# Delta attention and a mixture with slots: where the first passes prepare weights and slots, and where two tiles of maxima stand

## The chip, the cores and the metric

The kernel runs on one core of one Trainium2 chip. The metric is the time of one execution on the device in microseconds. Engines are TensorE (PE in the profile), VectorE (DVE), ScalarE (ACT), GpSimd (POOL) and SyncE (SP), which only issues DMAs here.

## What is computed

```python
# attention, on layer-normed x: 4 sequences of 2048 tokens, D = 256, C = 128
k = k / max(norm(k), 1e-12)
trans = a_t * (I - b_t * kkT)
S = einsum('bij,bjk->bik', S, trans) + b_t * vkT
o = einsum('bc,bcd->bd', q_t, S) * g_t
x = x + (o @ Wo + bo)
# mixture of 8 x 128 slots, on layer-normed x
xn = rms_norm(x, gamma_x);  se = rms_norm(slot_embeds, gamma_slot)
logits   = einsum('bsd,etd->bset', xn, se)
dispatch = softmax(logits, axis=1)          # over the tokens
slots    = einsum('bsd,bset->betd', xn, dispatch)
processed = gelu(slots @ w1) @ w2
combine  = softmax(logits.reshape(b, s, e * t), axis=-1)
x = x + einsum('bnd,bsn->bsd', processed, combine)
```

## The kernel before

The attention works on 16 chunks of 128 tokens, each for all four sequences at once. Within a chunk the recurrence becomes a triangular system: M of a chunk is the product of its keys with themselves, scaled by decays (`system`, L582 on VectorE, its matmuls L1137 on TensorE). M goes to DRAM and comes back repeated over partitions (`blocks_out`, `blocks_in` on SyncE), and VectorE solves its diagonal blocks of 16 columns in 15 pairs of small operations (`product`, L596, and `column`, L607), which I call the base system. GpSimd spreads the result into Z (`spread_blocks`, L464), and three doublings on TensorE, ScalarE and VectorE (`turn_Z`, `products`, `doubling`, L621 and L624) complete the inverse. From it come the updates, the next state, the scores and the outputs.

Every engine has its own order of work, written out by hand in a function `step(i, q)`, called for i from -4 to 15. One step takes a base system of chunk i + 2, M of chunk i + 3, the projections of chunks i + 3 and i + 4, outputs of chunk i + 1 and the normed result of chunk i. `steps` unrolls i = -4 to -1, runs i = 0 to 11 in a hardware loop of six times two steps, and unrolls 12 to 15; with `first=1` it unrolls 0 and 1 too. An engine works strictly in its order; between engines semaphores hold it. `at` is i where it is a number of Python, and so in the unrolled steps alone.

VectorE's step consists of a first part with the base system, in between which stand biases (L555), weights, next states and the gated product (L645), and of a tail: input statistics, residual (L655), decays by scans (L564, L571), M (L582), the first doubling, the low part `Xl` of the normed result (L686), right side, second doubling, statistics, low parts of the turned input (L548) and the last doubling. GpSimd's step starts once M of a chunk is there: residual addition (L414), a cut of M by a mask (L448), decayed keys kTg (L436) and queries qTg (L443), the other cut, a half cut (L456), then small norms, Z (L464) and the spread of beta (L430).

The mixture's weights are prepared within attention's first steps, on VectorE. `mixture_weights(1)` scales w1 by gamma (step -3), `(2)` writes the high fp16 part of w2 (step -3, L700), `(3)` that of w1 and `(4)` the low part of w2 (step -2, ahead of the base system, L703 and L706), `(5)` the low part of w1 (tail of step -2, L710). `slots_scaled` scales the eight groups of slot embeddings by their norms and gammas (L718), `slots_high` casts them to fp16 (L724); both stand ahead of the base system of step -1, and `slots_low` (L728) in its tail. The slots are turned on TensorE in step 13.

At the end, TensorE computes the first half of batch 0's logits in steps 14 and 15 and after (`early_logits`), ScalarE copies them out of PSUM into L (L1061), and VectorE takes column maxima `cmax` and row maxima `rmax` of each tile of 128 tokens (`early_maxima`, L846, L849, L850): tiles 0 to 2 in the tail of step 15, tiles 3 to 15 after the last step. The mixture goes on with the second half of the logits; it turns `cmax` on TensorE (L1923), reduces it on VectorE (`m_mcol`, L1591) and spreads it on TensorE (L1929).

## Time and profile before

| | us |
|---|---|
| median of three runs (1187.94, 1190.2, 1190.31) | 1190.2 |
| the profiled execution | 1187.25 |
| its span, first to last instruction | 1185.4 |
| TensorE busy | 1113.2 (94%) |
| VectorE busy | 938.2 (79%) |
| ScalarE busy | 735.6 (62%) |
| GpSimd busy | 314.5 (27%) |
| mean granted clock of TensorE | 0.985 of full speed |

All times of rows are microseconds from the start of the span. The timeline lists an engine's instructions in their order; a bracket behind one tells how long the engine stood idle before it, and what released it. A duration contains what the instruction waits for within the engine, so that the same operation can have several durations. An end is a start and a duration added.

### The profile page before, as it was taken

The page shows a single profiled execution, that of the slowest core. Times are in us where ns is not written, and L with a number is a line of the kernel's source. Part 1 is how long each engine was busy: PE and PEld are TensorE (multiplying, and loading weights), DVE is VectorE, ACT ScalarE, POOL GpSimd, SP SyncE. Part 2 cuts the span into 40 slices and gives each one's busy share as a digit, 9 for nine tenths or more (in the row PEclk, how much of TensorE's full clock was granted, in tenths as well). Part 3 has the DMA queues.
Part 4 walks back from the last instruction along what each step waited for, and adds up shares of the span by engine and source line. Part 5 has one row for each costly group of instructions (what it writes and reads, how often), then busy time and mean ns, then how long its engine had stood idle before and what let it go on. Part 6 is the DMA issues. An engine that isn't in the chain of part 4 may idle for free.

```text
span 1185.4 us, 26905 instructions
## 1 busy us (share of the span) xinstructions
PE 1113.2 (94%) x8600; PEld 854.5 (72%) x8600; DVE 938.2 (79%) x2195; ACT 735.6 (62%) x1385; POOL 314.5 (27%) x389
## 2 busy tenths in 40 slices
PE   4489999999999889899999999999999999999998
PEld 2378888888888764587786486787486787487787
DVE  4789888888889747997586898576898666998665
ACT  3446567665766445687663697664587664497763
POOL 3647656676567611000021000022000022000012
PEclk9699999999999989999999999999999999999999
DMA  6113432233233343232273031264031355000155
GB/s 191 45 45 81 125 98 85 87 107 119 80 88 95 99 96 100 66 72 57 55 170 78 2 72 45 63 147 103 2 72 32 74 123 130 0 1 1 22 119 128
DMA packets 185519, 94.02 MB, mean 79 GB/s; under 512 B 123680, under 2 KB 176928, under 8 KB 185440
## 3 DMA queue, kind: packets, MB, share of 16 engines
q1 hardware_dynamic: 178384, 75.40, 26.6%
q0 software_dynamic: 5792, 17.05, 4.9%
q8 instruction: 49, 0.80, 0.3%
q10 hardware_dynamic: 1264, 0.53, 0.2%
q14 instruction: 30, 0.25, 0.1%
HBM read 38.42 MB, written 29.36 MB: 57 GB/s over the span
## 4 chain that ended last, share of the span: by engine, by line
PE 66%; DVE 16%; issue 11%; ACT 4%; POOL 2%; DMA 1%; DVEq 1%; SPq 0%; ACTq 0%; POOLq 0%
PE m_wide L2015 14%; PE m_wide L1992 7%; PE m_wide L1978 7%; PE m_wide L1898 6%; PE a_bank L1095 4%; DVE m_Dm L1598 3%; PE a_bank L1107 3%; PE a_bank L1157 2%; DVE m_El L1606 2%; PE m_wide L2003 2%; ACT m_Eh L1781 2%; PE a_bank L1233 2%; PE a_bank L1146 2%; DVE cmax L1569 2%; PE m_wide L1952 2%
## 5 line engine op out<-in xcount | busy, mean ns | idle before, releaser
L1536 POOL DMA_DIRECT2D out_dram<-m_o x64 | 35.4, 553 | 627.1 <-DVE m_o L1720 514.3
L1952 PE MATMUL m_wide<-m_X,m_Eh 128*128 128x257 f16 (+1 forms) x1024 | 171.5, 273 | 2.7 <-DVE m_El L1606 2.7
L1898 PE MATMUL m_wide<-seT,XT 128*128 128x512 f16 x672 | 147.3, 379 | 0.9 <-issue 0.8
L2015 PE MATMUL m_wide<-m_Ph,m_Th 128*128 128x257 f16 x512 | 140.4, 274 | 4.3 <-DVE m_Pl L1645 4.3
L1952 PE MATMUL m_wide<-m_X,m_El 128*128 128x257 f16 (+1 forms) x512 | 139.7, 273 | 0.0
L2015 PE MATMUL m_wide<-m_Ph,m_Tl 128*128 128x257 f16 x512 | 139.4, 272 | 0.0
L2015 PE MATMUL m_wide<-m_Pl,m_Th 128*128 128x257 f16 x512 | 139.1, 272 | 0.0
L1898 PEld LDWEIGHTS m_wide<-seT,XT 128*128 (+1 forms) x672 | 65.5, 98 | 78.5 <-ACT L L1754 1.5
L1952 PEld LDWEIGHTS m_wide<-m_X,m_Eh 128*128 128x128 f16 x1024 | 99.2, 98 | 20.8 <-DVE m_El L1606 3.8
L1754 ACT COPY L<-m_wide 128x512 f32<-128x512 f32 (+1 forms) x112 | 65.1, 584 | 78.6 <-PE m_wide L1898 77.8
L1774 ACT ACTIVATE m_E<-m_Dm,m_eshift 128x512 f32<-128x512 f32 x128 | 92.5, 722 | 23.5 <-DVE m_Dm L1598 22.5
L1817 ACT COPY m_Tl<-m_wide 128x1024 f16<-128x1024 f16 x64 | 64.7, 1011 | 66.1 <-PE m_wide L2003 66.1
L1606 DVE TENSOR_TENSOR m_El<-m_E,m_Eh 128x512 f16<-128x512 f32 x128 | 87.7, 688 | 7.2 <-ACT m_Eh L1781 3.3
L1598 DVE TENSOR_TENSOR m_Dm<-L,m_Mb 128x512 f32<-128x512 f32 x128 | 87.6, 684 | 0.0
L1569 DVE TENSOR_TENSOR cmax<-cmax,L 128x512 f32<-128x512 f32 x112 | 77.1, 689 | 9.7 <-ACT L L1754 6.3
L1992 PE MATMUL m_wide<-w2s,m_hh 128*128 128x256 f16 x512 | 84.5, 273 | 0.0
L1978 PE MATMUL m_wide<-m_sTh,w1s 128*128 128x512 f16 x256 | 77.5, 379 | 0.0
L1781 ACT CAST m_Eh<-m_E 128x512 f16<-128x512 f32 x128 | 77.0, 605 | 0.0
L1575 DVE TENSOR_REDUCE rmax<-L 128x1 f32<-128x512 f32 (+1 forms) x112 | 76.0, 679 | 0.0
L1811 ACT ACTIVATE L<-L,m_nrm (+1 forms) x64 | 73.7, 1151 | 0.9 <-DVE m_nrm L1640 0.9
L1992 PE MATMUL m_wide<-w2s,m_hl 128*128 128x256 f16 x256 | 69.8, 273 | 0.0
L1631 DVE TENSOR_TENSOR m_hl<-m_E,m_hh 128x512 f16<-128x512 f32 x64 | 43.9, 691 | 24.6 <-ACT m_hh L1802 24.5
(198 smaller groups left out, 2712.5 us busy)
## 6 DMA issues: line engine op xcount, KB each, us to landing
L<-in_L_attn_x_dram SPq DMA_DIRECT2D x16, 512.0 KB, 7.2
Mrep<-M_dram SPq DMA_DIRECT2D x32, 256.0 KB
x_dram<-x SPq DMA_DIRECT2D x16, 512.0 KB, 6.6
m_X<-X_dram SPq DMA_DIRECT2D x128, 64.0 KB, 1.8
m_x1t<-x_dram POOLq DMA_DIRECT2D x32, 256.0 KB, 3.5
out_dram<-m_o POOLq DMA_DIRECT2D x64, 128.0 KB, 2.4
M_dram<-M_ SPq DMA_DIRECT2D x16, 256.0 KB, 2.6
X_dram<-Xh SPq DMA_DIRECT2D x16, 256.0 KB, 2.3
```

Of the source, the lines that this page charges most:

```text
L1569: dve.tensor_tensor(cmax[:, half_at], cmax[:, half_at], L[:, z, bass.ds(tile, 1), :] .rearrange("q a n -> q (a n)"), ALU.max).then_inc(cm_ ...
L1575: dve.tensor_reduce(rmax[:, bass.ds(z * NT + tile, 1)], L[:, z, bass.ds(tile, 1), :] .rearrange("q a n -> q (a n)"), AX.X, ALU.max, negate ...
L1598: dve.tensor_tensor(Dm[p][:, :], L[:, v, bass.ds(4 * g + t, 1), :] .rearrange("q a n -> q (a n)"), Mb[:, v * HS:(v + 1) * HS], ALU.subtrac ...
L1606: dve.tensor_tensor(El[t % 4][:, :], E[t % 4][:, :], Eh[t % 4][:, :], ALU.subtract)\
L1774: act.activation(E[t % 4][:, :], Dm[p][:, :], ACT.Exp, bias=eshift[:, 0:1]).then_inc(E_ok[p], 1)
L1781: act.copy(Eh[t % 4][:, :], E[t % 4][:, :]).then_inc(Eh_ok[p], 1)
L1811: act.activation(row, row, ACT.Exp, bias=nrm[:, bass.ds(4 * k + t, 1)]).then_inc(Ec_ok, 1)
L1898: last = pe.matmul(lg[t % 4], XT[:, sx * KD + k, bass.ds((4 * g + t) * P, P)], seT[:, ss, k, z * HS:(z + 1) * HS], start=(c == 0), stop=(c ...
L1952: last = pe.matmul(acc[v][q], e[t % 4][:, qs], X[:, sx, bass.ds(4 * g + t, 1), 0:XW].rearrange("q a n -> q (a n)"), start=first and e is E ...
L1978: last = pe.matmul(up[f % 2], w1s[:, sw, k, f * P:(f + 1) * P], sT[ss][:, k, :], start=(c == 0), stop=(c == 3 * KD - 1))
L1992: last = pe.matmul(down[q % 2], hT[sh][:, f, q * P:(q + 1) * P], w2s[:, sw, f, :], start=(c == 0), stop=(c == 3 * NF - 1))
L2015: last = pe.matmul(co[p], a, pp[:, e, 0:XW], start=(c == 0), stop=(c == 3 * NS - 1))
```

## The change

On GpSimd, the low part of w2 is made at the end of step -3 (`second_weights_low`: w2 is scaled in place, and its high part subtracted); in step -2 the key norms and the spread of beta of chunk 1 come ahead of and behind the residual addition instead of near the end. On VectorE, `mixture_weights(4)` is gone, `(3)` stands behind the decays of step -2, the scaled slots stand in two halves of four in the tails of steps -1 and 0, the high part in the tail of step 1, and the low part in that of step 12. Its steps 0 and 1 are unrolled. On ScalarE and TensorE the keys and the system of chunk 1 come ahead of Z of chunk 0 in step -2. The memset and tile 0 of the maxima stand behind the weights in step 14, tile 1 behind the gated product, and tiles 2 to 5 in the tail of step 15.

```diff
--- before.py
+++ after.py
@@ -478,8 +478,14 @@
             def step(i, q):
                 r = 1 - q
                 at = i if isinstance(i, int) else None
+                if at == -2:
+                    if live(i + 3):
+                        key_norms(i + 3)
                 if live(i + 2):
                     residual(i + 2, q)
+                if at == -2:
+                    if live(i + 3):
+                        spread_beta(i + 3)
                 if live(i + 2):
                     cut(i + 2, q, 1)
                 if live(i + 2):
@@ -491,16 +497,23 @@
                     half_cut(i + 2, q)
                 if live(i):
                     output_norm(i)
-                if live(i + 3):
+                if live(i + 3) and at != -2:
                     key_norms(i + 3)
                 if live(i + 2):
                     spread_blocks(i + 2, q)
-                if live(i + 3):
+                if live(i + 3) and at != -2:
                     spread_beta(i + 3)
                 if live(i + 4):
                     norm(i + 4)
                 if at == -3:
+                    second_weights_low()
                     slot_norms()
+
+            def second_weights_low():
+                pool.wait_ge(w2h_ok, 1)
+                pool.tensor_scalar(w2_in, w2_in, WSCALE, None, ALU.mult).then_inc(w2h_ok, 1)
+                pool.wait_ge(w2h_ok, 2)
+                pool.tensor_tensor(w2s[:, 1, :, :], w2_in, w2s[:, 0, :, :], ALU.subtract).then_inc(w2h_ok, 1)
 
             def slot_norms():
                 pool.wait_ge(sq_ok, 1)
@@ -701,23 +714,21 @@
                 elif step == 3:
                     dve.wait_ge(w1_ok, 1)
                     dve.tensor_copy(w1s[:, 0, :, :], w1_g).then_inc(w1_ok, 1)
-                elif step == 4:
-                    dve.wait_ge(w2h_ok, 1)
-                    dve.scalar_tensor_tensor(w2s[:, 1, :, :], w2_in, WSCALE, w2s[:, 0, :, :],
-                                             ALU.mult, ALU.subtract)
                 elif step == 5:
                     dve.wait_ge(w1_ok, 2)
                     dve.tensor_tensor(w1s[:, 1, :, :], w1_g, w1s[:, 0, :, :], ALU.subtract).then_inc(w1_ok, 1)
 
-            def slots_scaled():
-
-                dve.wait_ge(srn_ok, 1)
-                dve.wait_ge(w1_ok, 3)
-                dve.wait_ge(gxs_ok, 1)
-                for e in range(NS):
+            def slots_scaled(first, past):
+                if first == 0:
+                    dve.wait_ge(srn_ok, 1)
+                    dve.wait_ge(w2h_ok, 3)
+                    dve.wait_ge(w1_ok, 3)
+                    dve.wait_ge(gxs_ok, 1)
+                for e in range(first, past):
                     last = dve.scalar_tensor_tensor(slots_g[:, e, :], slots_in[:, e, :], srn[:, e:e + 1], gxs[:, :],
                                                     ALU.mult, ALU.mult)
-                last.then_inc(slots_ok, 1)
+                if past == NS:
+                    last.then_inc(slots_ok, 1)
 
             def slots_high():
                 dve.wait_ge(slots_ok, 1)
@@ -748,11 +759,6 @@
                         biases(i + 3, r, 3)
                     if live(i + 3):
                         biases(i + 3, r, 1)
-                    mixture_weights(3)
-                    mixture_weights(4)
-                if at == -1:
-                    slots_scaled()
-                    slots_high()
                 for s in range(BS - 1):
                     if live(i + 2):
                         product(i + 2, s)
@@ -767,6 +773,8 @@
                     if s == 8:
                         if live(i + 1):
                             weights(i + 1, r)
+                        if at == NCH - 2:
+                            early_maxima(0)
                     if s == 10:
                         if live(i + 1) and live(i + 2):
                             next_state(i + 1, r, 0)
@@ -778,6 +786,8 @@
                     if s == 12:
                         if live(i + 1):
                             gated(i + 1, r)
+                        if at == NCH - 2:
+                            early_maxima(1)
                 if live(i + 2):
                     columns_done(i + 2)
                 if live(i + 4):
@@ -801,6 +811,8 @@
                     decays(i + 3, r, 1)
                 if at == -3:
                     mixture_weights(2)
+                if at == -2:
+                    mixture_weights(3)
                 if live(i + 3):
                     system(i + 3, r)
                 if live(i + 3):
@@ -812,9 +824,15 @@
                 if at == -2:
                     mixture_weights(5)
                 if at == -1:
+                    slots_scaled(0, NS // 2)
+                if at == 0:
+                    slots_scaled(NS // 2, NS)
+                if at == 1:
+                    slots_high()
+                if at == NCH - 4:
                     slots_low()
                 if at == NCH - 1:
-                    for t in range(3):
+                    for t in range(2, 6):
                         early_maxima(t)
                 if live(i):
                     low_part(i)
@@ -849,8 +867,8 @@
                 dve.tensor_tensor(cmax[:, 0:HS], cmax[:, 0:HS], L[:, 0, t, :], ALU.max).then_inc(cm_ok, 1)
                 dve.tensor_reduce(rmax[:, t:t + 1], L[:, 0, t, :], AX.X, ALU.max, negate=True).then_inc(rm_ok, 1)
 
-            steps(dve, step)
-            for t in range(3, NT):
+            steps(dve, step, first=1)
+            for t in range(6, NT):
                 early_maxima(t)
 
         @block.scalar
@@ -1014,11 +1032,14 @@
                     keys(i + 3, r)
                 if live(i + 3):
                     gates(i + 3, r)
+                if at == -2:
+                    if live(i + 3):
+                        turned_keys(i + 3)
                 if live(i + 2):
                     turned_Z(i + 2, 0)
                 if at == NCH - 3:
                     turned_slots((0,))
-                if live(i + 3):
+                if live(i + 3) and at != -2:
                     turned_keys(i + 3)
                 if live(i + 2):
                     products(i + 2, 0)
@@ -1274,17 +1295,23 @@
                     outputs(i + 1, at == NCH - 2)
                 if live(i + 3):
                     spread_alpha(i + 3)
+                if at == -2:
+                    if live(i + 3):
+                        turn_keys(i + 3, r)
+                if at == -2:
+                    if live(i + 3):
+                        system(i + 3)
                 if live(i + 2):
                     turn_Z(i + 2, q, 0)
                 if at == NCH - 3:
                     turn_slots((0,))
-                if live(i + 3):
+                if live(i + 3) and at != -2:
                     turn_keys(i + 3, r)
                 if live(i + 2):
                     products(i + 2, q, 0)
                 if at == NCH - 3:
                     turn_slots((1,))
-                if live(i + 3):
+                if live(i + 3) and at != -2:
                     system(i + 3)
                 if live(i + 2):
                     doubling(i + 2, q, 0)
```

## Rows read from the trace of the kernel before

**Rows 1.** The page, part 4: the chain that ended last, by engine.
```profile
PE 66%; DVE 16%; issue 11%; ACT 4%; POOL 2%; DMA 1%; DVEq 1%; SPq 0%; ACTq 0%; POOLq 0%
```

**Rows 2.** VectorE's timeline, 27 to 53 us: start, duration, engine, line, operation.
```profile
27.03 1.20 DVE L700 TENSOR_SCALAR w2s<-seT 128x2048 f16<-128x2048 f32 x1
...
37.60 1.22 DVE L703 CAST w1s<-L 128x2048 f16<-128x2048 f32 x1
38.74 4.44 DVE L706 SCALAR_TENSOR_TENSOR w2s<-seT,w2s 128x2048 f16<-128x2048 f32 x1
43.10 1.27 DVE L596 TENSOR_TENSOR tmp<-Mrep,a_const 128x60 f32<-128x60 f32 x1
44.41 1.19 DVE L607 TENSOR_TENSOR Zc<-a_const,tmp 128x60 f32<-128x60 f32 x1
...
47.41 0.21 DVE L596 TENSOR_TENSOR tmp<-Mrep,Zc 128x52 f32<-128x52 f32 x1
...
52.99 0.17 DVE L607 TENSOR_TENSOR Zc<-Zc,tmp 128x4 f32<-128x4 f32 x1
```

**Rows 3.** VectorE's timeline, 59 to 74 us.
```profile
59.38 0.69 DVE L582 TENSOR_TENSOR M_<-a_bank,gamb_ 128x512 f32<-128x512 f32 x1 [2.25 <-PE a_bank L1137]
...
61.60 2.27 DVE L710 TENSOR_TENSOR w1s<-L,w1s 128x2048 f16<-128x2048 f32 x1
...
69.15 3.24 DVE L718 SCALAR_TENSOR_TENSOR L<-XT,srn,gxs 128x256 f32<-128x256 f32 x8
...
73.57 0.21 DVE L596 TENSOR_TENSOR tmp<-Mrep,a_const 128x60 f32<-128x60 f32 x1
```

**Rows 4.** GpSimd's timeline beside the first base system.
```profile
40.99 3.31 POOL L448 TENSOR_TENSOR L<-M_,a_const 128x512 f32<-128x512 f32 x1
44.26 1.26 POOL L436 TENSOR_TENSOR kTg_<-kT,gbc_ 128x512 f32<-128x512 f32 x1
```

**Rows 5.** Stretches: length, each engine's busy time, TensorE's clock, DMA share, GB/s.
```profile
38.00:38.50 0.50, 0.50 (x4) 0.26 (x3) 0.50 (x1) 0.50 (x5) 0.50 (x2) 1.00 0.03 8
78.70:82.10 3.40, 3.40 (x16) 3.14 (x15) 2.34 (x13) 0.87 (x3) 1.26 (x2) 0.50 0.00 0
```

**Rows 6.** GpSimd's timeline in the tail of step -1.
```profile
89.00 2.37 POOL L414 TENSOR_TENSOR L<-L,bo 128x1024 f32<-128x1024 f32 x1
```

**Rows 7.** VectorE's timeline in later steps.
```profile
82.55 0.69 DVE L645 TENSOR_TENSOR OT<-a_bank,gateT_ 128x512 f32<-128x512 f32 x1 [1.34 <-PE a_bank L1224]
...
91.25 2.27 DVE L728 TENSOR_TENSOR L<-L 128x2048 f16<-128x2048 f32 x1
...
116.04 2.29 DVE L686 TENSOR_TENSOR Xl<-xf,Xh 128x1024 f16<-128x1024 f32 x1
...
406.19 1.20 DVE L686 TENSOR_TENSOR Xl<-xf,Xh 128x1024 f16<-128x1024 f32 x1
...
409.58 0.42 DVE L621 TENSOR_TENSOR Z_<-Z_,a_bank 128x256 f32<-128x256 f32 x1 [0.95 <-PE a_bank L1170]
```

**Rows 8.** TensorE's timeline in step -1.
```profile
77.53 0.39 PE L1107 MATMUL a_bank<-L,wqg_h 128*128 128x512 f16 x1 [3.87 <-DVE L L555]
```

**Rows 9.** VectorE's timeline in steps 14 and 15.
```profile
449.70 0.69 DVE L645 TENSOR_TENSOR OT<-a_bank,gateT_ 128x512 f32<-128x512 f32 x1 [3.68 <-PE a_bank L1224]
451.95 1.45 DVE L655 TENSOR_TENSOR x<-L,a_bank 128x512 f32<-128x512 f32 x2 [1.57 <-PE a_bank L1233]
...
456.89 0.91 DVE L846 MEMSET cmax<- 128x1024 f32 x1 [0.16 <-issue]
...
461.88 1.22 DVE L686 TENSOR_TENSOR Xl<-xf,Xh 128x1024 f16<-128x1024 f32 x1 [0.29 <-ACT Xh L973]
```

**Rows 10.** TensorE's timeline at the start of the mixture.
```profile
478.10 0.66 PE L1923 MATMUL m_wide<-ident,cmax 128*128 128x128 f32 x4 [1.61 <-DVE cmax L849]
...
484.07 0.65 PE L1929 MATMUL m_wide<-ident,m_mcol 128*128 128x128 f32 x4 [1.43 <-DVE m_mcol L1591]
```

## The prediction

> **What bounds the kernel now.** I read the page first. Its chain of the work that ended last lies on TensorE for 66% of the span and on VectorE for 16% [rows 1]. Then I went through attention in order of time, engine by engine. The attention part is a pipeline of 20 steps, of 24.2 us each once it runs (from Xl at 116.04 to Xl at 406.19 in twelve). From step 0 on VectorE hardly rests in one, so an edit counts where it lengthens or shortens VectorE's series of work. The first steps run otherwise. In step -2 VectorE's first base system starts at 43.10, behind a cast and a 4.44 us operation [rows 2]. In step -1 the second one starts at 73.57, behind 4.4 us of slot work from 69.15 on [rows 3]. In the first the reader is to see two late starts, in the second a wait on TensorE of 2.25 us before M of chunk 1 at 59.38.
>
> The rows of GpSimd beside these [rows 4] show what I take to decide the case. VectorE's operation at 38.74 needs some 2.2 us (the one of the same size at 61.60 took 2.27 [rows 3]) and took 4.44: it began to run at about 41.0, where GpSimd's addition ended and its cut was issued, and ended at 43.18. That cut, 1.26 us of work as the kTg behind it, took 3.31 us and ended at 44.30. VectorE's product of 60 columns took 1.27 us instead of 0.21 (at 47.41 [rows 2]) and ended 0.07 us later, at 44.37; the column update behind it took 1.19 us and ended at 45.60, just after GpSimd's kTg. Two more follow in the same way. So two operations that both read two operands of SBUF exclude each other, and a waiting one gets its turn as soon as the other engine's single operation ends. Operations of VectorE that take one operand from PSUM, and the statistics, run through. The pairs give two prices: after GpSimd's operation VectorE's ends its own length less 0.13 us later (0.07 for 0.21), and then GpSimd's of 512 elements ends some 1.13 us later (43.18 to 44.30).
>
> **Step -3 and -2.** Removed ahead of the first base system: the cast (1.2 us) and the low part of w2 (4.44 us). It can start at 37.7, where the cast did; its matrix is there by then but for its end, for the DMA engines fall silent at 38 [rows 5]. GpSimd now scales w2 (2048 elements, one operand) and subtracts. No row has that size there: from the addition's 1024 elements in 2.37 us [rows 6] the subtraction is some 4.6 us, the scaling between 2 us (half of the rate of the same row) and 4.6 us. The first starts once the high part is written, at 28.2 (27.03 and 1.20 us [rows 2]), and the second ends between 35 and 37.6. In that stretch each operation of VectorE has an operand in PSUM (M, the scans, low parts and biases), so I cost them at nothing; if they took 2 us more, they would hold the first base system by as much. The Trainium skill (Perfetto Trace Analysis, Optimizing Scalar/DVE Operations) says that moving work between VectorE and GpSimd may not help, for they share a port. By that rule up to 4.6 us would come back here; by the rows, with nothing of two SBUF operands beside it, none does.
>
> GpSimd's key norms of chunk 1 now stand ahead of its addition. They wait for ScalarE's four squares, which start when VectorE's last bias is done at 37.6; with a maximum and a power behind them I put 2.7 us for all, an estimate, so that the addition starts at about 40.3. Where it starts moves little: it blocks VectorE for the same time. Queued behind it are the spread of beta, two cuts, kTg and a half cut: 2.25 + 4 x 1.13 + 0.6, a good 7.5 us with VectorE's turns. The base system needs 6.75 us alone (26 operations from 47.41 to 53.16 and the first four at 0.25). During the 7.5 us it gets one operation in after each of six, 1.4 us of work. So it ends at 37.7 + 6.75 + 6.1 = 50.6 instead of 53.16: 2.6 us gained out of 5.6 removed. Z of chunk 0 goes with it.
>
> Keys and system of chunk 1 now run on TensorE while it waits for that Z, and its wait of 2.25 us on M goes. The 6.2 us from 53.16 to 59.38 become 6.2 - 2.25 + 1.2 (the cast) = 5.1, so M of chunk 1 comes at 55.7, 3.7 us sooner. SP's store and the two broadcasts follow it and are no wait. VectorE's last w1 part then meets GpSimd's addition or cut, and ends at about 61.1 instead of 63.87 [rows 3]: 2.8 us sooner. The doubling behind it moves along.
>
> **Step -1.** The slot scaling and the high part (69.15 to 73.57, 4.4 us) leave the place ahead of the second base system. It starts at 69.15 - 2.8 = 66.4, which is 7.2 us sooner. The wait of 1.34 us for the gated product at 82.55 [rows 7] came from TensorE being late (its wait of 3.87 us [rows 8], then 1.2 GHz for 3.4 us [rows 5]) and goes too. That makes -8.5 at the end of this base.
>
> In the tail the low slot part (2.27 us, 91.25) gives way to four scalings. Each takes 0.405 us alone (3.24 for eight [rows 3]), and each has two SBUF operands. They arrive as GpSimd's addition ends (89.00 + 2.37 = 91.37 [rows 6]), with a cut, kTg, qTg and a cut queued. The four end at 91.37 + 4 x 0.27 + 3 x 1.13 = 95.84 against 93.52: +2.3.
>
> **Step 0.** The other four stand ahead of Xl (116.04 [rows 7]), which took 2.29 us instead of 1.20 (406.19) since it waited for a cut, and ended at 118.33. So that cut ended 1.07 us before, at 117.26. From there four times 0.27, four operations of GpSimd (3 x 1.13 and a half cut's 0.5) and Xl's 1.07 give 123.3: +4.9. If they come just ahead of the cut, 4.4.
>
> **Step 1.** The cast of the slots (1.2 us, by the one at 37.60) and one GpSimd operation that gets in before Xl: +2.3; I take +2.0, since a short wait of VectorE behind it, as the one of step 12 below, can take up a little.
>
> **Step 12.** The low slot part (2.2 us) ahead of Xl (406.19), then kTg, then Xl: Xl ends at 410.6 instead of 407.39. VectorE waited 0.95 us at 409.58 [rows 7], so +2.3. No wait later in attention absorbs it: what follows hangs on that doubling.
>
> Alone, without GpSimd in between, these four places cost -0.6, +1.6, +1.2 and +1.3. The bounds of each are these and the above.
>
> **Clock.** TensorE now idles 5 to 6 us in the tail of step 0. In the trace an idle stretch of 3.87 us was followed by 3.4 us at 1.2 GHz [rows 5, 8], which cost the 1.34 us above. I take one such stretch: +1.3; bounds 0 and four.
>
> **The maxima.** The memset and tile 0 now run after the weights, tile 1 after the gated product of the last chunk: VectorE's waits of 3.68 us at 449.70 and of 1.57 us at 451.95 [rows 9] hide the 2.1 and 1.2 us. In the last step memset and three tiles fill 456.89 to 461.6 (0.9 and 3.7 us, so 1.2 a tile), and four tiles end at 461.7, just before the wait of 0.29 us on Xh is over. So ten instead of thirteen tiles remain after Xl, 1.2 us each: 3.6 us. TensorE waits for them at 478.10 (1.61 us) and for the column maxima at 484.07 (1.43 us) [rows 10] and is full from there on. So it gets 3.0 of the 3.6: -3.0.
>
> **Sum.** -8.5 + 2.3 + 4.9 + 2.0 + 2.3 + 1.3 - 3.0 = +1.3. The profiled execution took 1187.25 us (span 1185.4), so it would take 1188.5. The median of the runs shown is 2.95 us higher; on that scale it is 1191.5. A measurement of this kernel can tell 0.2%, 2.4 us, from nothing. This is within it.
>
> **Rivals.**
> *The scalings keep the port.* They follow each other with no semaphore, and GpSimd may not get in between. For it: no row shows back-to-back operations of one line against GpSimd. Against: the addition got in between the cast and the 4.44 us operation, which also stood back to back. Then the four places cost the lower figures and no gap opens that lowers the clock: -8.5 - 0.6 + 1.6 + 1.2 + 1.3 - 3.0 = -8.0, or 1182.2. The Trainium skill (SBUF — State Buffer, Who interferes with whom) says that whoever starts first has the shared pair for the whole instruction and the other blocks. It does not say who is next; read for a series it would give this time. The trace agrees on the lock (4.44 us at 38.74). Chance 0.32.
> *Slower: the clock.* The tails of steps -1, 0, 1 and 12 all open gaps of some 2 us or more on TensorE; if each is followed by a stretch at 1.2 GHz for 1.34 us, the sum is +1.3 + 3 x 1.34 = +5.3, or 1195.5. It decides from the second on. Against it: each gap but step 0's is shorter than the 3.87 us. Chance 0.09.
> *GpSimd's w2 part isn't hidden:* at the rate of its cut it runs past 37.7, and the first base system starts up to 2 us later: +3.3, or 1193.5. Chance 0.05.
>
> **Chances and range.** My forecast has 0.54, its own range is 1187 to 1195: 0.05 of it faster by over 0.2%, 0.32 within, 0.17 slower. With the rivals: faster 0.05 + 0.32 = 0.37; within 0.32 + 0.02 = 0.34; slower 0.17 + 0.09 + 0.03 = 0.29. The range takes in the first rival and the slow one: 1181 to 1195.5.
>
> **What would show it.** Right: the first base system starts near 37.7 and ends near 50.6 with six stretched operations; M of chunk 1 near 55.7; the second base system near 66.4; scalings of some 1.4 us from one to the next with GpSimd's between; no wait on cmax at TensorE. Wrong: scalings 0.4 us apart; a base system that ends before 49 or after 52; 1.2 GHz in other tails; a wait on XT or L in place of the one on cmax.

## The result, and the profile after

The changed kernel took 1197.07 us (median of four runs, 1196.84 to 1197.58) beside 1189.92 us of the kernel before: a ratio of 1.0069, interval 1.0053 to 1.0085. That is 7.15 us slower, and 1197.07 lies outside my range of 1181 to 1195.5. The profiled execution of it took 1197.58 us, with a span of 1196.0 us. That is 10.6 more than the span profiled before, which came from one of the faster runs of that kernel.

The page after, part 1 (busy time) and part 4 (the chain that ended last, by engine):

```profile
PE 1123.4 (94%) x8600; PEld 863.4 (72%) x8600; DVE 946.3 (79%) x2194; ACT 736.8 (62%) x1385; POOL 324.5 (27%) x391
...
PE 71%; DVE 13%; issue 8%; ACT 4%; POOL 3%; DMA 1%; DVEq 0%; ACTq 0%; SPq 0%; POOLq 0%
```

TensorE is busy 10.2 us longer than before, with the same matmuls to do, and its share of the chain went from 66% [rows 1] to 71%. The same multiplications took longer. The view of stretches says where. I cut attention where a base system starts, so that each row is one step. First the kernel before, then the changed one. The columns are length, busy time of TensorE, weight loads, VectorE, ScalarE and GpSimd (number of instructions in brackets), TensorE's granted clock, DMA share and GB/s.

```profile
43.10:73.57 30.47, 18.55 (x144) 16.45 (x144) 24.52 (x66) 10.58 (x25) 18.97 (x18) 0.78 0.20 59
73.57:99.42 25.85, 20.90 (x148) 17.21 (x148) 22.70 (x77) 10.63 (x30) 15.24 (x15) 0.93 0.23 62
99.42:124.24 24.82, 23.61 (x188) 19.95 (x186) 22.16 (x77) 15.47 (x40) 15.36 (x18) 1.00 0.31 88
124.24:148.46 24.22, 23.70 (x189) 19.99 (x187) 21.57 (x77) 15.48 (x40) 15.56 (x18) 1.00 0.34 102
```

```profile
36.19:67.57 31.38, 21.37 (x124) 17.47 (x125) 24.37 (x58) 10.38 (x29) 24.42 (x22) 0.73 0.23 59
67.57:95.99 28.42, 25.02 (x186) 20.77 (x184) 24.30 (x80) 12.85 (x35) 14.52 (x15) 0.93 0.24 66
95.99:129.48 33.49, 27.52 (x186) 22.65 (x185) 27.14 (x81) 15.51 (x40) 15.00 (x18) 0.81 0.25 71
129.48:158.43 28.95, 26.67 (x187) 22.24 (x186) 23.71 (x78) 15.52 (x40) 15.86 (x18) 0.88 0.28 83
158.43:183.16 24.73, 23.52 (x186) 19.76 (x184) 22.06 (x77) 15.60 (x40) 15.32 (x18) 1.00 0.29 82
```

The reader is to see steps 0 and 1 (third and fourth row). They ran at a clock of 1.00 before and run at 0.81 and 0.88 now. TensorE is busy 3.9 and 3.0 us longer in them with as many matmuls, and they last 8.67 and 4.73 us longer. The whole difference of the two spans, in such stretches:

| stretch | before | after | difference | predicted |
|---|---|---|---|---|
| start to VectorE's last bias before chunk 0 | 37.69 | 36.27 | -1.42 | 0 |
| from there to the second base system | 35.88 | 31.30 | -4.58 | -7.2 |
| step -1 | 25.85 | 28.42 | +2.57 | +1.0 |
| step 0 | 24.82 | 33.49 | +8.67 | +6.2 |
| step 1 | 24.22 | 28.95 | +4.73 | +2.0 |
| step 2 | 24.01 | 24.73 | +0.72 | 0 |
| steps 3 to 11 | 217.44 | 217.42 | -0.02 | 0 |
| step 12 | 23.52 | 26.98 | +3.46 | +2.3 |
| step 13 to the first turn of cmax | 64.66 | 65.21 | +0.55 | -1.6 |
| from there to the end | 707.33 | 703.24 | -4.09 | -1.4 |
| sum | | | +10.6 | +1.3 |

VectorE's timeline after, which answers to [rows 2, 3, 7]:

```profile
36.19 0.25 DVE L609 TENSOR_TENSOR tmp<-Mrep,a_const 128x60 f32<-128x60 f32 x1
...
53.81 0.69 DVE L595 TENSOR_TENSOR M_<-a_bank,gamb_ 128x512 f32<-128x512 f32 x1
...
56.98 0.42 DVE L634 TENSOR_TENSOR Z_<-Z_,a_bank 128x256 f32<-128x256 f32 x1 [1.84 <-PE a_bank L1191]
...
67.57 0.21 DVE L609 TENSOR_TENSOR tmp<-Mrep,a_const 128x60 f32<-128x60 f32 x1
...
83.90 4.68 DVE L728 SCALAR_TENSOR_TENSOR L<-XT,srn,gxs 128x256 f32<-128x256 f32 x4
...
113.71 5.72 DVE L728 SCALAR_TENSOR_TENSOR L<-XT,srn,gxs 128x256 f32<-128x256 f32 x4
119.35 1.63 DVE L699 TENSOR_TENSOR Xl<-xf,Xh 128x1024 f16<-128x1024 f32 x1
...
148.69 2.29 DVE L699 TENSOR_TENSOR Xl<-xf,Xh 128x1024 f16<-128x1024 f32 x1
...
419.02 2.29 DVE L699 TENSOR_TENSOR Xl<-xf,Xh 128x1024 f16<-128x1024 f32 x1
```

GpSimd's timeline after: the two new operations on w2, and what stood beside the scalings at 83.90 (it answers to [rows 4, 6]).

```profile
26.82 5.39 POOL L514 TENSOR_SCALAR seT<-seT 128x2048 f32<-128x2048 f32 x1
32.28 4.08 POOL L516 TENSOR_TENSOR w2s<-seT,w2s 128x2048 f16<-128x2048 f32 x1
...
83.97 1.52 POOL L448 TENSOR_TENSOR L<-M_,a_const 128x512 f32<-128x512 f32 x1
85.45 1.45 POOL L436 TENSOR_TENSOR kTg_<-kT,gbc_ 128x512 f32<-128x512 f32 x1
86.86 1.44 POOL L443 TENSOR_TENSOR qTg_<-qT_,gbc_ 128x512 f32<-128x512 f32 x1
88.26 1.44 POOL L448 TENSOR_TENSOR L<-M_,a_const 128x512 f32<-128x512 f32 x1
```

Four scalings of 0.405 us each take 4.68 and 5.72 us. Beside them GpSimd's operations follow each other every 1.4 us, one after each scaling. That is the alternation I had forecast, and the rival in which the scalings keep the port is out. By the port I mean whatever makes two operations that both read two operands of SBUF exclude each other, as in these rows.

TensorE's timeline after: step -2, the tails of steps -1, 0, 1 and 12, and the start of the mixture (it answers to [rows 10]).

```profile
46.36 2.07 PE L1158 MATMUL a_bank<-kT 128*128 128x128 f32 x8 [4.46 <-ACT kT L943]
...
90.81 0.66 PE L1167 MATMUL a_bank<-a_const,Z_ 128*128 128x128 f32 x4 [3.11 <-DVE Z_ L634]
...
123.21 1.12 PE L1167 MATMUL a_bank<-a_const,Z_ 128*128 128x128 f32 x4 [5.70 <-DVE Z_ L634]
...
153.21 0.93 PE L1167 MATMUL a_bank<-a_const,Z_ 128*128 128x128 f32 x4 [2.02 <-DVE Z_ L634]
...
422.95 1.01 PE L1167 MATMUL a_bank<-a_const,Z_ 128*128 128x128 f32 x4 [2.75 <-DVE Z_ L634]
...
492.77 0.60 PE L1950 MATMUL m_wide<-ident,cmax 128*128 128x128 f32 x4
...
497.09 0.60 PE L1956 MATMUL m_wide<-ident,m_mcol 128*128 128x128 f32 x4
```

Eight matmuls took 2.07 us behind an idle stretch of 4.46 us, and four took 1.12 behind 5.70, where the same four took 0.66 in the step before. Behind the gaps of 2.02 and 2.75 us they took 0.93 and 1.01. The turns of cmax and of the column maxima no longer have a bracket: they wait for nothing that the profile shows.

### The profile page after: what moved, and what is told of

Read it like the earlier page. It is cut to its first block, busy times and chain, and to the rows that moved or that the text cites. A ratio compares the mean times of both kernels' runs of the same rounds, so it can differ in the third digit from the quotient of the medians.

```text
span 1196.0 us, 26871 instructions
## 1 busy us (share of the span) xinstructions
PE 1123.4 (94%) x8600; PEld 863.4 (72%) x8600; DVE 946.3 (79%) x2194; ACT 736.8 (62%) x1385; POOL 324.5 (27%) x391
## 4 chain that ended last, share of the span: by engine, by line
PE 71%; DVE 13%; issue 8%; ACT 4%; POOL 3%; DMA 1%; DVEq 0%; ACTq 0%; SPq 0%; POOLq 0%
PE m_wide L2042 14%; PE m_wide L1925 11%; PE m_wide L2019 7%; PE m_wide L2005 7%; PE a_bank L1116 4%; DVE m_Dm L1625 3%; PE a_bank L1128 3%; DVE m_El L1633 2%; PE m_wide L2030 2%; ACT m_Eh L1808 2%; PE a_bank L1178 2%; PE a_bank L1254 2%; PE a_bank L1167 2%; PE m_wide L1979 2%; PE a_bank L1218 1%
```

## The experiments

My theory once the traces were there: the port terms are right, and the loss beyond them is TensorE's clock, which stands at 1.2 GHz behind the gaps that the scalings make. The rivals were the amount of work itself and w2 on GpSimd. The kernels ran on several chips, so I compare each with the kernel before on its own chip by the ratio, and the steps by the traces. Where I give microseconds under the changed kernel, they are plain differences of medians, across chips. The lengths of steps, with the time in them at 1.2 GHz in brackets, for the kernels below (us; the first column runs from the end of the last bias to the second base system, and holds 4.4 us of slot work in before, e1, e4, e6 and e12):

```
kernel              to step -1    step -1       step 0        step 1        step 12       to the end*
before              35.88 (13.7)  25.85 (3.4)   24.82 (0)     24.22 (0)     23.52         771.99
after               31.30 (17.1)  28.42 (4.0)   33.49 (13.0)  28.95 (6.9)   26.98         768.45
e9_after_again      30.94 (17.1)  28.45 (3.4)   31.05 (6.8)   27.30 (3.4)   27.09         768.12
e5_no_maxima        31.24 (17.1)  28.44 (3.9)   33.48 (13.0)  28.96 (7.0)   26.92         770.99
e4_maxima_only      36.55 (13.6)  26.79 (6.8)   24.83 (0)     24.22 (0)     23.51         768.89
e12_maxima_again    37.17 (17.1)  25.63 (3.4)   24.80 (0)     24.21 (0)     23.96         770.81
e1_slots_back       36.36 (17.1)  26.48 (6.8)   24.63 (0)     23.81 (0)     23.66         768.46
e6_step_m2_only     36.38 (17.1)  24.43 (0)     24.66 (0)     23.81 (0)     24.25         769.59
e2_slots_in_base    31.18 (17.1)  25.25 (0)     25.19 (0)     24.72 (0)     25.92         768.35
e10_in_base_again   31.09 (17.1)  25.24 (0)     25.19 (0)     24.71 (0)     25.94         769.03
e3_filler           31.03 (17.1)  26.93 (0)     29.51 (0)     25.81 (0)     26.63         766.92
e7_filler_m2        28.64 (3.4)   25.24 (0)     25.19 (0)     24.73 (0)     26.03         770.15
e8_half_in_tail     30.60 (17.1)  25.24 (0)     32.09 (10.2)  25.42 (3.4)   25.50         766.71
e11_low_early       31.29 (17.1)  25.24 (0)     25.19 (0)     28.45 (3.4)   23.52         767.45
                    * from the start of the last base system (step 13)
```

**e1: the slots back ahead of step -1's base system**, the low part in its tail; all else as changed.

```
-                if at == -1:
-                    slots_scaled(0, NS // 2)
...
+                if at == -1:
+                    slots_scaled(0, NS)
+                    slots_high()
                 for s in range(BS - 1):
```

> The changed kernel with the slot work put back: all eight scalings and the high part ahead of the base system of step -1, the low part in the tail of step -1; all else as changed. My theory: the loss sits in the slot work, which in the tails alternates with GpSimd's operations (3.1, 4.5, 1.1 and 1.1 us of waiting by the changed trace) and opens gaps on TensorE that are followed by 1.2 GHz. So the second base system starts 4.4 us later than in the changed kernel, but the two stretches at 1.2 GHz after 92 and 119 are gone, and the time falls by about 10 us, to 2 or 3 us under the kernel before (the maxima's 2 to 3 us, with next to nothing from step -2). Rival, the reordered step -2 or VectorE's unrolled steps are at fault: the time stays within 3 us of the changed kernel. Rival, it is the mere amount of VectorE work in the later tails: the same fall of 10 us, so this run alone doesn't tell it from mine; the run with the slots in the base does.

Measured: 1181.55 us, ratio 0.9928 (0.991 to 0.9945), 15.5 us under the changed kernel. Steps 0 and 1 are back at 24.63 and 23.81 us. The loss sits in the moved slot pieces. I had expected a fall of 10 us. Between the two profiled executions it is 15.4 us: 14.2 from the last bias to the last base system, 1.2 in the load, and nothing behind.

**e2: the four pieces inside the base systems** of the same steps, behind their second column, where GpSimd is idle. The work on VectorE is the same, the neighbour is not.

```
+                    if s == 1:
+                        if at == -1:
+                            slots_scaled(0, NS // 2)
+                        if at == 0:
+                            slots_scaled(NS // 2, NS)
+                        if at == 1:
+                            slots_high()
+                        if at == NCH - 4:
+                            slots_low()
```

> The changed kernel with each of the four pieces of slot work in the same step but inside the base system, behind its second pair of operations, where GpSimd stands idle. VectorE does the same work in the same step. My theory (the port): four scalings take 1.6 us instead of 4.7 and 5.7, the cast 1.2, the low part 2.2, Xl 1.2 or 2.3; no gap of more than 1 us ahead of TensorE's second turn of Z. The four pieces cost 1.6 + 1.6 + 1.2 + 2.2 = 6.6 us where they cost some 20 now, so the time falls by 10 to 13 us, to 3 to 6 us under the kernel before. Rival, the amount of work: nothing but the place within a step has changed, so the time stays within 3 us of the changed kernel. Rival, the gaps only move (TensorE waits for the weights' product instead) and are followed by 1.2 GHz as well: the waits of VectorE go but 1.2 GHz stays in steps 0 and 1, and the fall is 6 us or less.

Measured: 1181.03 us, ratio 0.9922 (0.9902 to 0.9942). VectorE's timeline, and the stretches of steps -1, 0 and 1:

```profile
69.06 1.67 DVE L728 SCALAR_TENSOR_TENSOR L<-XT,srn,gxs 128x256 f32<-128x256 f32 x4
```

```profile
68.12:93.36 25.24, 23.91 (x187) 19.72 (x185) 21.46 (x80) 12.92 (x35) 13.29 (x15) 1.00 0.23 62
93.36:118.56 25.20, 23.93 (x187) 19.79 (x185) 22.79 (x82) 15.47 (x40) 15.32 (x18) 1.00 0.31 89
118.56:143.28 24.72, 23.86 (x186) 19.72 (x184) 22.78 (x79) 15.47 (x40) 16.38 (x18) 1.00 0.29 86
```

Four scalings take 1.67 us instead of 4.68 and 5.72, the clock stays at 1.00, and steps 0 and 1 are 8.3 and 4.2 us shorter than in the changed kernel. So the amount of work isn't the cause. Alternation and clock together are; what each is worth, the next one tells. By its ratio e2 is no faster than e1: both undo the loss, and the slots gain nothing from their new places.

**e3: unused matmuls in TensorE's gaps.** The changed kernel, with 26, 50 and 16 matmuls of 256 columns into a free part of a bank ahead of the third turn of Z in steps -1, 0 and 1. They add no result. TensorE's steps 0 and 1 are unrolled for it, which no run tests by itself.

```
+                if at in (-1, 0, 1):
+                    filler({-1: 26, 0: 50, 1: 16}[at])
                 if live(i + 2):
                     turn_Z(i + 2, q, 2)
```

> The changed kernel with matmuls of no use (256 columns, into an unused half of a PSUM bank) ahead of TensorE's second turn of Z in steps -1, 0 and 1: 26, 50 and 16 of them, sized to fill its gaps of 3.1, 5.7 and 2.0 us. TensorE's steps 0 and 1 are unrolled for it. My theory: VectorE's waits stay as they are (four scalings still take 4.7 and 5.7 us), but TensorE's clock stays at 2.4 GHz from 61 to 420; the step from the third to the fourth base system falls from 33.5 to about 30 us, the one before from 28.4 to about 26.5, the one behind from 29.0 to 27.5. In all 6 to 7 us less than the changed kernel, so about as fast as the kernel before. Rival, the slower steps have nothing to do with the clock (the waits on TensorE behind the gaps are late starts): the step lengths stay within 0.5 us, and so does the time.

Measured: 1187.51 us, ratio 0.9981 (0.997 to 0.9992), 9.6 us under the changed kernel. TensorE's timeline in step 0, and the stretches of steps -1 to 1:

```profile
115.43 5.62 PE L1370 MATMUL a_bank<-wkv_h 128*128 128x256 f16 x50
121.31 0.66 PE L1167 MATMUL a_bank<-a_const,Z_ 128*128 128x128 f32 x4 [0.25 <-DVE Z_ L634]
```

```profile
68.54:95.47 26.93, 26.35 (x213) 22.33 (x211) 24.31 (x81) 12.82 (x35) 14.11 (x15) 1.00 0.24 70
95.47:124.98 29.51, 28.97 (x237) 24.68 (x235) 26.90 (x82) 15.48 (x40) 15.00 (x18) 1.00 0.28 82
124.98:150.79 25.81, 25.26 (x203) 21.34 (x201) 23.44 (x79) 15.49 (x40) 16.31 (x18) 1.00 0.30 84
```

The four matmuls that took 1.12 us behind the gap take 0.66, and the clock is 1.00 in all three steps. The steps are 1.49, 3.98 and 3.14 us shorter: 8.6 us is what the clock cost there, as far as the filler changed nothing else. VectorE's busy time, with the scalings against GpSimd, is as in the changed kernel. What is left over the kernel before goes with the port: +1.08, +4.69 and +1.59, where I had +1.0, +4.9 and +2.0. (The first contains the wait of 1.34 us that goes, the last some 0.4 us that VectorE's unrolled step 1 saves, below.)

**e4 and e12: the maxima alone**, on the kernel before; the same kernel on two chips.

```
                     if s == 8:
...
+                        if at == NCH - 2:
+                            early_maxima(0)
...
-                    for t in range(3):
+                    for t in range(2, 6):
```

> The kernel before with the maxima's part of the change alone: memset and tile 0 behind the weights of step 14, tile 1 behind the gated product, tiles 2 to 5 in the tail of step 15. My theory: TensorE's waits of 1.6 us on cmax and 1.4 us on the column maxima go and nothing takes their place, 3.0 us faster than the kernel before (2 to 3.5). Rival, the gain in the changed kernel was eaten by 1.2 GHz after 484 and would be here too: 1.9 us or less. Rival, VectorE or ScalarE is the bound of the first dispatch: both waits go, but the dispatch starts at most 1 us sooner.

> The kernel before with the maxima part alone, once more. My prediction priced it at 3.0 us (three waits of 1.61, 1.43 and part of 0.95). The first time it came out at 7.1 by medians and some 1.7 between the profiled executions. If 3.0 is right, the ratio is 0.9965 to 0.9985; if something else is gained with it, 0.994 again.

Measured: 1182.75 us, ratio 0.994 (0.9924 to 0.9957) the first time, and 1187.41 us, ratio 0.9987 (0.9974 to 1.0) the second. TensorE's timeline in the second:

```profile
479.61 0.60 PE L1927 MATMUL m_wide<-ident,cmax 128*128 128x128 f32 x4
```

No wait on cmax in either. From the last base system to this turn the first took 63.02 us against 64.66 before. That is 1.64 less, the wait's size; the second took 65.13. By the view of stretches TensorE had 10.0 us at 1.2 GHz there in the first and 15.2 in the second, with the same code. The two results lie 5 us apart for one kernel, and their intervals don't touch: an interval of a ratio covers the scatter within one set of runs and not that between chips. So the 7.1 us of the first were no size of this part, and single ratios that differ by less than 0.5% don't rank two kernels here.

**e5: the changed kernel without its maxima part.**

> The changed kernel with the maxima part alone undone: tiles 0 to 2 all in the last pass behind the last system, as before. If the maxima part is worth the three waits that its rows show (3.0 us), this is 3 us over the changed kernel, about 1200. If it is worth the 7.1 us by which it alone moved the kernel before, it is about 1204, and the rest of the change is then worth about +14.

Measured: 1200.3 us, ratio 1.0097 (1.0073 to 1.0122), against 1.0069 with it: 0.0028, or 3.3 us. The edit is e4's undone. The size is near my 3.0, but the two intervals overlap, and the waits in this trace are 0.48 us on cmax and 1.43 on the column maxima, 1.9 in sum. From the last base system to the end the part is worth 2.5 us between these two profiled executions, 3.1 in e4, 1.2 in e12 and 1.1 between e6 and e1. It gains; how much stays open between these.

**e6: step -2's part alone**, on the kernel before (this is e1 with the maxima as before; VectorE's steps 0 and 1 stay unrolled in it).

> The kernel before with the changes of step -2 alone (second chunk's turned keys and system first, w2's low part on GpSimd, its cast behind the base system, the slots where they were, the maxima as before). My prediction had this part at 2.8 and 1.34 us of gain: 4.1 under the kernel before, about 1185.8. The rival, that TensorE at 1.2 GHz in step -2 takes the gain back: within 1.5 us of the kernel before.

Measured: 1184.14 us, ratio 0.9959 (0.9945 to 0.9973): 4.9 us under the kernel before by the ratio, as forecast for the part. The trace doesn't bear the forecast's working out, though. From the last bias to the second base system it took 36.38 us, not less than the 35.88 of before. Only step -1 is shorter, by the gated product's wait (25.85 to 24.43), and that too is no property of the part: e1 has the same code up to step 14, took 26.48 us there with 6.8 us at 1.2 GHz, where e6 had none, and its gated product waited 1.98 us. From the last bias to the last base system it is 375.6 us, before 375.8. What the profiled execution gained lies in the load, whose last bias was done at 35.20 us instead of 37.69, and behind step 13 (2.4 us). So size and reason don't agree, and what this part is worth in the median stays open.

**e7: unused matmuls in step -2**, on e2: 40 ahead of the second chunk's system, 20 behind it.

```
+                    filler(40)
                     if live(i + 3):
                         system(i + 3)
+                    filler(20)
```

> The kernel with the four slot pieces inside the base systems (1181.0), with 40 unused matmuls (256 columns, 0.11 us each at 2.4 GHz) ahead of the second chunk's system in step -2 and 20 behind it, in TensorE's idle stretches of 4.5 and 2.5 us. If the granted clock of 0.50 from 44.7 to 61.8 us is what took step -2's gain back, the clock stays at 1.0 there and the time falls by 2 to 3 us, to about 1178.5. If the order of the work on VectorE sets step -2 anyway, the time stays within 1 us of 1181.

TensorE's timeline and the stretch of step -2:

```profile
42.75 4.53 PE L1371 MATMUL a_bank<-wkv_h 128*128 128x256 f16 x40
47.39 1.16 PE L1159 MATMUL a_bank<-kT 128*128 128x128 f32 x8
48.38 2.35 PE L1371 MATMUL a_bank<-wkv_h 128*128 128x256 f16 x20
```

```profile
37.73:66.45 28.72, 24.43 (x184) 20.00 (x185) 24.57 (x58) 10.47 (x29) 24.10 (x21) 0.94 0.22 64
```

The eight matmuls of keys take 1.16 us instead of 2.07, the clock of the step is 0.94 instead of 0.73, and it lasts 28.72 us against 31.26 in e2. The first base system starts at 37.73 and the second at 66.45: my prediction had 37.7 and 66.4. So step -2's plan was right for a TensorE mostly at 2.4 GHz, and 2.5 us of it (against e2) were lost to 1.2. The match to 0.1 us has some luck in it: M came at 55.27, 0.4 us ahead of the forecast, and the rest took as much longer, with 3.4 us at 1.2 GHz left in it. The time doesn't show it: 1184.59 us, ratio 0.9966 (0.9954 to 0.9979), which is worse than e2's by 0.0044. The profiled execution had its first turn of cmax 3.5 us sooner than e2's, and gave 3.7 us back in the mixture. From that turn to the end, the view of waits lists 4.3 us in four waits of TensorE without a releaser, and 1.6 us in three in e2. This row has one of them, of 1.78 us:

```profile
651.96 4.26 PE L1932 MATMUL m_wide<-seT,XT 128*128 128x512 f16 x19 [1.78 <-issue]
```

**e8: one piece in the tail.** e2, with the second four scalings left in step 0's tail.

```
                     if s == 1:
...
-                        if at == 0:
-                            slots_scaled(NS // 2, NS)
...
+                if at == 0:
+                    slots_scaled(NS // 2, NS)
```

> The changed kernel with only the second four scalings left in the tail of the pass of step 0, the other three pieces inside the base systems. Against 1181.0 with all four inside: the alternation with GpSimd alone (5.72 for 1.62 us) would add 4.1, to about 1185; alternation and a stretch at 1.2 GHz behind the gap it makes add 7 to 8, to about 1188.5.

Measured: 1186.06 us, ratio 0.9978 (0.9968 to 0.9988), which is 0.0056 or 6.7 us above e2's by the ratios and 5.0 by the bare medians. The forecasts were 4.1 for the alternation alone and 7 to 8 with the clock, so the time alone doesn't tell them apart. The steps do: step 0 is 6.90 us longer than in e2 and step 1 0.70, 7.6 in all, with 10.2 and 3.4 us at 1.2 GHz. The port's part of it is 5.72 - 1.67 = 4.05, the rest is the clock's and what waited behind.

**e9 and e10: the changed kernel and e2 once more**, side by side with e11 and e12.

> The changed kernel itself once more, beside the next three on one chip. The time behind the recurrence differed by up to 4 us between kernels whose mixture is the same code, with waits for which the profile shows no releaser. If that is scatter from run to run, the ratio to the kernel before stays at 1.007 within 0.002 and the single runs spread over several us, as those of the kernel before do. If the changed kernel is free of these waits by its layout, its runs stay within 1 us of each other.

> The four slot pieces inside the base systems, once more. The ledger of base-system starts says 16 us less than the changed kernel at chunk 15 and the same from there on: 1181, a ratio to the kernel before of 0.992 to 0.993. If the earlier result was a lucky draw of four runs, it comes out near 1184.

Measured: 1195.43 us, ratio 1.0064 (1.0041 to 1.0088), and 1180.2 us, ratio 0.9928 (0.9905 to 0.9952). Both come out again, on another chip. The runs of the changed kernel spread over 2.8 us, those of the kernel before over 8.6 us. The repeated trace holds a comparison that no edit could give. Steps 0 and 1 of the same kernel:

```profile
97.73:128.78 31.05, 25.07 (x187) 20.91 (x185) 26.95 (x81) 15.49 (x40) 14.99 (x18) 0.89 0.26 77
128.78:156.08 27.30, 25.01 (x186) 20.81 (x185) 23.48 (x78) 15.49 (x40) 16.30 (x18) 0.94 0.30 88
```

VectorE and GpSimd are busy as long as in the first trace within 0.5 us, but there were 6.8 and 3.4 us at 1.2 GHz instead of 13.0 and 6.9, and the steps are 2.44 and 1.65 us shorter. One us at 1.2 GHz costs 0.4 to 0.5 us here (2.44 for 6.2, 1.65 for 3.5), and 0.3 between e1 and e6 (2.05 for 6.8).

**e11: the low part in step 1 too**, behind the high part, inside the base system (e2 without its piece in step 12).

```
                         if at == 1:
                             slots_high()
-                        if at == NCH - 4:
                             slots_low()
```

> As the kernel with the four pieces inside the base systems, but the slots' low part also in step 1, right behind the high part, and nothing in step 12. The low part's 2.27 us moves from step 12 to step 1. If step 12 lost only that (25.9 us against 24.2 in the kernel with step -2 alone is 1.7), the total stays within 0.5 us. If its stretch at 1.2 GHz (409.9 to 423.6, against 10.2 us without the piece) costs beside it, up to 1 us is gained. A loss would say that GpSimd is not idle long enough in step 1: with alternation 2.27 would become some 5.

Measured: 1182.09 us, ratio 0.9948 (0.9929 to 0.9966), 1.9 us over e10: a miss. Step 12 gained 2.4 us as the part left (25.94 to 23.52). But step 1 lost 3.7 for 2.27 us of work. TensorE's timeline has the reason: the two pieces in a row hold VectorE's biases back, and the gap was followed by 3.4 us at 1.2 GHz.

```profile
126.47 0.39 PE L1128 MATMUL a_bank<-L,wqg_h 128*128 128x512 f16 x1 [2.83 <-DVE L L568]
```

e2 beats both kernels, the kernel before by 0.7 to 0.8%, in both of its results. So does e1, by 0.7%.

## Why the prediction was wrong

**Port.** Right in kind and size. The four scalings of step -1 took 4.68 us (I had 95.84 - 91.37 = 4.5), those of step 0 with Xl ran from 113.71 to 120.98, which is 4.98 longer than Xl's 2.29 alone (I had 4.9). In steps 1 and 12 Xl came out at 2.29 us behind one GpSimd operation, as forecast. The rival with the higher chance of a gain (0.32) rested on the order in a series and fell by 83.90 and 113.71. The Trainium skill (SBUF — State Buffer, Who interferes with whom) has the lock, and the trace agrees (4.68 and 5.72 us for four scalings of 0.405). Who comes next it leaves open; here it was strict alternation in both tails.

**w2 on GpSimd.** All but hidden in the changed kernel, as said: its second operation ended at 36.36, between my bounds, and the base system started at 36.19 with a product of 0.25 us. The scaling took 5.39 us, over my upper bound of 4.6; the subtraction took 4.08, under its 4.6. The cover is thin. In e1 and e6, whose last bias was done near 35.1, the first product took 1.5 us.

**Base system 0.** From 36.19 to 49.32, 13.1 us against my 12.9, with six stretched operations.

**Step -2.** The step "its wait of 2.25 us on M goes" was right (M at 53.81 has no bracket), and "2.8 us sooner" failed. TensorE ran 17.1 us of this step at 1.2 GHz, 13.7 in the trace before; e12, whose step -2 is that of before, had 17.1 too and took 1.3 us longer there, so the extra 3.4 us aren't the change's own. VectorE now waited 1.84 us for TensorE at 56.98, and more behind. I moved the second chunk's system to where TensorE idles, but never asked at what clock it would do it. With the gaps filled (e7) the forecast of the second base system came out.

**Clock.** This is the step that failed: "I take one such stretch: +1.3; bounds 0 and four". By the fillers it was 1.5 in step -1, 4.0 in step 0 and 3.1 in step 1, 8.6 us in the profiled execution, and 2.5 more in step -2 (e7 against e2). In the second trace of the changed kernel steps -1 to 1 took 4.1 us less, so it varies. The bounds failed in two ways. I set the smallest gap that counts at the 3.87 us of [rows 8]; behind the tails of steps -1 and 1 stretches of 3.4 to 6.8 us at 1.2 GHz followed, where TensorE had stood idle 3.11 and 2.02 us. And I took each for 3.4 us at 1.34 us, from one row [rows 5], while step 0's ran 13.7 us. The trace before could have warned me: it has stretches of 13.7 us from 44.5 and of 6.8 from 413 as well, and in the 13 us ahead of the latter no single wait of TensorE was over 0.6 us. So the length of one gap doesn't tell what follows. The slow rival named the mechanism (each gap followed by 1.2 GHz) at +5.3, with a chance of 0.09; its places were right but for step -2, which it lacked, and its +5.3 was half of the +10.6 that came.

**Step 2 and 12.** Step 2 is 0.7 us longer in every kernel in which VectorE's step 1 stands unrolled, and step 1 some 0.4 shorter (24.22 to 23.81 in e1 and e6). I hadn't asked what the unrolling does. Step 12 has +3.46 for my +2.3. The port came out there (from the low slot part to Xl's end 4.47 us, 3.27 more than Xl's 1.20; I had 3.2), and TensorE's gap of 2.75 us was followed by 1.2 GHz from 423.0 on, 4.5 us of it in this step, with a wait of 2.69 us on TensorE at its end. No run filled this gap, so the clock's share isn't shown.

**Maxima.** Right in kind: the waits of [rows 10] are gone. The size lies between 1.1 and 3.1 us by the traces. From the last base system to the turn of cmax the changed kernel took 0.55 us longer instead of 1.6 less. TensorE had 16.0 us at 1.2 GHz there, 10.0 before: the stretch behind step 12's gap runs on to 433.5, that of step 14 is 6.8 us instead of 3.4, and there is a new one (484.5 to 488.0, where the logits wait for XT). e5 has all three, so they don't come from the maxima. What they cost isn't shown; e4 and e12, one kernel, differ by 2.1 us there for 5.2 us at 1.2 GHz. I had named XT; its wait was there before, at 2.37 us, and is 2.54 now.

**What I couldn't have read.** From the first turn of cmax to the end the code is the same in all kernels, and took 702.9 to 707.3 us in the profiled executions. The three with the order of attention of before have 705.7 to 707.3, the others all but e7 702.9 to 705.2. The profile has waits without a releaser there. What they are stays open; no run was made for it. With them, and with a load that ended between 35.0 and 38.3 us, single kernels carry 2 us or more that no step explains, as e4, e6 and e7 show. The clock has its part in this too: where two kernels run the same code, their time at 1.2 GHz still differs (e4 and e12, e1 and e6).

## What to carry to other kernels

Before moving work of two SBUF operands on VectorE, list what GpSimd has queued at the new place: in these tails each such operation paid for one of GpSimd's. The same four scalings cost 1.67 us beside an idle GpSimd and 5.72 us beside a queue. Then follow the delay to TensorE, because a gap there is paid twice, once as time and again at half the clock; where the gap can't be closed, unused matmuls in it are worth trying (9.6 us in e3; in e7 they shortened their step, and the whole kernel got no faster). Price a clock term from every stretch at 1.2 GHz in the trace, the longest too, and not from a single one.

## What the runs showed of the hardware that I had not expected

GpSimd's scaling of 2048 fp32 elements per partition with one operand (5.39 us) took longer than its subtraction with two operands into fp16 (4.08 us).

The same kernel got 13.0 us at 1.2 GHz in step 0 in one execution and 6.8 in another, with the same instructions ahead of it. So the length of such a stretch is no property of the code alone. The kernel before also had 6.8 us at 1.2 GHz from 413 on, with no single wait of TensorE over 0.6 us in the 13 us ahead of it.

Filling TensorE's gap with matmuls that nobody reads kept the granted clock at 1.00 in steps -1 to 1 (e3), and in step 0 they delayed nothing: the turn of Z behind them still waited 0.25 us for VectorE.
